# Attention in two halves: full groups for batch 0, groups of 256 queries for batch 1, on one core

## The reference, cut to what matters

```python
# x: 2 x 1024 x 512, eight heads of eight dimensions
qk = (x @ Wqk.T + bqk)             # split into q and k per head
v  = (x @ Wv.T + bv)
scores = q k^T                     # per head, 1024 x 1024
attn = softmax(scores) / 8
x = layernorm(x + (attn v) @ Wo.T + bo)
# feed-forward, int4 weights with a scale for each group of 128 inputs
h = silu(x @ Wg.T) * (x @ Wu.T)    # 512 -> 1792
x = layernorm(x + h @ Wd.T)        # 1792 -> 512
```

## Time and profile before

| | |
|---|---|
| median of 3 runs | 521.45 us (521.42 to 521.49) |
| the profiled execution | 521.81 us, its span 519.7 us |
| granted clock of TensorE, mean | 0.998 |
| PE busy | 501.1 us (96%), 2976 matmuls |
| DVE busy | 413.0 us (79%) |
| ACT busy | 405.5 us (78%) |
| POOL busy | 255.7 us (49%) |

### The profile page before, as it was taken

One profiled execution on the slowest core, in us unless ns is written; L12 is line 12 of the kernel. 1 busy time (PEld: TensorE's weight loads), 2 busy tenths in 40 slices (PEclk: granted clock), 3 DMA queues, 4 the chain that ended last, 5 costly groups with the idle time before them and its releaser, 6 DMA issues.

```text
span 519.7 us, 8086 instructions
## 1 busy us (share of the span) xinstructions
PE 501.1 (96%) x2976; PEld 193.2 (37%) x2976; DVE 413.0 (79%) x705; ACT 405.5 (78%) x558; POOL 255.7 (49%) x295
## 2 busy tenths in 40 slices
PE   8899999999999999999999999999999999999994
PEld 3222222323222322234444444444444444444441
DVE  3699999989999997368878778778668666788677
ACT  1522888998899989877888888888888888888880
POOL 9100091823100715073464676664997962648741
PEclk9999999999999999999999999999999999999999
DMA  6410018576530005700031121140020020000022
GB/s 192 136 68 5 21 35 211 182 144 125 91 59 1 3 5 103 276 7 1 1 59 24 20 43 21 20 62 1 1 81 1 0 83 0 3 0 1 0 81 81
DMA packets 30151, 29.20 MB, mean 56 GB/s; under 512 B 19489, under 2 KB 21921, under 8 KB 29857
## 3 DMA queue, kind: packets, MB, share of 16 engines
q1 hardware_dynamic: 26688, 22.67, 15.7%
q0 software_dynamic: 3424, 6.03, 6.3%
HBM read 24.37 MB, written 4.23 MB: 55 GB/s over the span
## 4 chain that ended last, share of the span: by engine, by line
PE 79%; DVE 7%; POOL 5%; ACT 5%; issue 2%; DMA 1%; SPq 0%; DVEq 0%; POOLq 0%; ACTq 0%
PE ps L1123 16%; PE ps L1135 16%; PE ps L1157 16%; PE ps L1068 9%; PE ps L1039 6%; PE ps L963 6%; DVE mxh L1249 4%; ACT pbuf L760 3%; PE ps L892 3%; POOL x L617 2%; PE ps L1051 1%; PE ps L902 1%; PE ps L1016 1%; POOL stack L663 1%; DMA arena<-xT 1%
## 5 line engine op out<-in xcount | busy, mean ns | idle before, releaser
L1249 DVE TENSOR_REDUCE mxh<-ps 128x1 f32<-128x512 f32 x256 | 157.0, 680 | 6.5 <-PE ps L963 5.3
L760 ACT ACTIVATE pbuf<-ps,gamma 128x1024 f32<-128x1024 f32 x128 | 140.5, 1114 | 16.2 <-PE ps L1039 11.2
L841 ACT ACTIVATE ps<-ps,ratio 128x512 f32<-128x512 f32 x168 | 106.5, 659 | 40.4 <-PE ps L1123 37.3
L1157 PE MATMUL ps<-wd,stack 128*128 128x512 f16 x440 | 129.7, 379 | 0.7 <-POOL stack L663 0.6
L1123 PE MATMUL ps<-arena,wg 128*128 128x512 f16 x448 | 115.5, 379 | 0.1
L1135 PE MATMUL ps<-arena,wu 128*128 128x512 f16 x448 | 115.3, 379 | 0.1
L1423 DVE TENSOR_TENSOR ps<-ps,stack 128x512 f32<-128x512 f32 x128 | 87.8, 695 | 33.4 <-PE ps L1157 31.7
L847 ACT ACTIVATE ps<-ps,ratio 128x512 f32<-128x512 f32 x156 | 98.9, 659 | 6.6 <-PE ps L1135 2.3
L661 POOL CAST stack<-pbuf 128x512 f16<-128x512 f32 x55 | 33.5, 609 | 76.5 <-DVE pbuf L1398 76.5
L1423 DVE TENSOR_TENSOR ps<-ps,pbuf 128x512 f32<-128x512 f32 x76 | 52.6, 695 | 23.2 <-PE ps L1157 22.5
L1068 PE MATMUL ps<-pbuf,arena 128*32 128x256 f32 x832 | 66.5, 391 | 1.7 <-ACT avt L767 1.7
(11 more groups left out here) (120 smaller groups left out, 387.4 us busy)
## 6 DMA issues: line engine op xcount, KB each, us to landing
arena<-xT SPq DMA_DIRECT2D x16, 256.0 KB, 5.8
x<-x SPq DMA_DIRECT2D x2, 2048.0 KB, 10.0
out<-x SPq DMA_DIRECT2D x3, 1024.0 KB, 4.2
stack<-down_ratios SPq DMA_DIRECT2D x1, 2048.0 KB, 9.6
wg<-gq POOLq DMA_DIRECT2D x4, 448.0 KB, 7.3
wu<-uq POOLq DMA_DIRECT2D x4, 448.0 KB, 7.4
wd<-dq POOLq DMA_DIRECT2D x2, 896.0 KB, 10.3
pbuf<-down_ratios SPq DMA_DIRECT2D x1, 1536.0 KB, 6.2
```

Of the source, the lines that this page charges most:

```text
L760: nc.scalar.activation(pbuf[:, pi % 4, :].rearrange("p (a n) -> p a n", a=2), ps[:, at:at + 2, :], ACT.Exp, scale=gamma[:, n // (ALL // B) ...
L841: nc.scalar.activation(gbank[t % 2], gbank[t % 2], ACT.Copy, scale=gr[:, t % G, c:c + 1])\
L1157: mm = nc.tensor.matmul(bank[k], mparts[:, a, t % NM, k * P:(k + 1) * P], wd[:, i, :], start=(i == 0 and a == 0), stop=(a == 1), skip_grou ...
L1249: nc.vector.tensor_reduce(mxh[:, f % 2, qh, half:half + 1], ring_bank("first", n), AX.X, ALU.max)\
```

## The change

Batch 0's blocks keep groups of 512 queries with eight steps. The blocks of batch 1 are cut into groups of 256 queries with four steps, each of two key blocks, so there are 12 groups, and four more turns M and copies by `av_out`. `avt` is still transposed once for 512 queries (TURNS = 8), at steps 9, 17, 25, 34, 42, 50 and 58. From step 24 the first pass issues 3.5 units a step, one unit instead of two in the second pair of even steps; it ends with step 56, and `DRAIN` is 57. Narrow scores are four matmuls of 256 columns for two of 512. `av_whole` is replaced by two halves. The maxima of a group move in four DMAs instead of two, each with fewer rows. avT of the seventh turn is no longer aside but in the shared banks.

The guards and products of the scales go to GpSimd, the reciprocals stay on VectorE at steps 48 and 52. Block 0's statistics are taken in steps 38, 43, 46 and 51, its aggregation in step 52. The second bias is added in four operations, the down weights are loaded in two groups' places, and the residual products stand in periods 26, 27, 33 to 35 and 40 to 44.

```diff
-FG = HG * BT * 2
-FIRST = NB * NG * FG
+WIDE = [(u, g, 0, BT) for u in range(NB // 2) for g in range(NG)]
+NARROW = [(u, g, q, BT // 2) for u in range(NB // 2, NB) for g in range(NG) for q in (0, BT // 2)]
+GROUPS = WIDE + NARROW
+NF = len(GROUPS)
+TURNS = NB * NG
+UNIT0 = [sum(2 * HG * group[3] for group in GROUPS[:f]) for f in range(NF + 1)]
+STEP0 = [sum(2 * group[3] for group in GROUPS[:f]) for f in range(NF + 1)]
+FG = UNIT0[1]
+FIRST = UNIT0[NF]
 AHEAD = FG + 14
+SLOWER = STEP0[3]
...
+        def issued_before(n, pair):
+            return min(AHEAD + 4 * n + 2 * pair - max(0, n - SLOWER + 1) // 2, FIRST)
+
         def firsts_at(n, pair):
-            m = AHEAD + 4 * n + 2 * pair
-            return range(m, min(m + 2, FIRST))
+            return range(issued_before(n, pair), issued_before(n + pair, 1 - pair))
...
-            f, r = divmod(n + 3, KT)
-            if r == 0 and f < NB * NG:
-                return [("M", f, 0)]
-            f, r = divmod(n - 9, KT)
-            if r == 0 and 0 <= f < LASTF:
-                return [("avT", f, 0)]
+            if n + 3 in STEP0[1:NF]:
+                return [("M", STEP0.index(n + 3), 0)]
+            if n in AVT_AT:
+                return [("avT", AVT_AT.index(n), 0)]
...
-        DRAIN = ALL - 11
-        ASIDE = {DRAIN: ("attT", 1, 0), DRAIN + 1: ("wo", 1, 0), DRAIN + 3: ("wo", 1, 1), DRAIN + 4: ("avT", LASTF, 0),
-                 DRAIN + 6: ("attT", 2, 0), DRAIN + 7: ("wo", 2, 0), DRAIN + 9: ("wo", 2, 1)}
+        STATS0_AT = (38, 43, 46, 51)
+        AVT_AT = (9, 17, 25, 34, 42, 50, 58)
+        DRAIN = ALL - 7
+        ASIDE = {DRAIN: ("attT", 1, 0), DRAIN + 1: ("wo", 1, 0), DRAIN + 2: ("wo", 1, 1), DRAIN + 3: ("attT", 2, 0),
+                 DRAIN + 4: ("wo", 2, 0), DRAIN + 5: ("wo", 2, 1)}
...
-        RESIDUAL_AT = 28
+        RESIDUAL_AT = (26, 27, 33, 34, 35, 40, 41, 42, 43, 44)
...
-                for jj in range(2):
-                    r = ROWS * jj + MROW
-                    sp.dma_start(qs[b][r:r + 3, k, 2 * g:2 * g + 2, :],
-                                 mrows[6 * BT * jj:6 * BT * (jj + 1), f % 2, :]).then_inc(s_mld[g], 16)
+                for c in range(HG):
+                    r, t = ROWS * (c // 2) + MROW, 2 * g + c % 2
+                    sp.dma_start(qs[b][r:r + 3, k, t, q * P:(q + count) * P],
+                                 mrows[3 * count * c:3 * count * (c + 1), f % 2, :]).then_inc(s_mld[f % 4], 16)
...
-            for f in range(2, NB * NG):
+            for f in range(2, NF):
                 split_max(f)
                 if f == 2:
-                    add_bias(0)
-                if f in (2, 3, 4):
-                    load_weights(f)
-                if f == 6:
-                    add_bias(1)
+                    add_bias(0, N // P)
                 if f == 3:
                     for t in range(BT):
                         add_attention(0, t)
+                if f == 4:
+                    guard_scales()
+                if 5 <= f < 9:
+                    add_bias(N // P + 2 * (f - 5), 2)
+                if f in (2, 3, 4, 5):
+                    load_weights(f)
+                if f == 8:
+                    guard_down_scales()
+                if f == 9:
+                    scale_ratios()
+                if f == 10:
+                    down_ratios()
...
-                for j in range(2):
-                    rows, t = slice(ROWS * j, ROWS * (j + 1)), 2 * g + pair
-                    mm = nc.tensor.matmul(bank[at + j], ks[b][rows, t, kt * P:(kt + 1) * P],
-                                          qs[b][rows, k, t, :], start=True, stop=True)
+                for i in range(BT // count):
+                    kt = BT // count * (n - STEP0[f]) + i
+                    for j in range(2):
+                        rows, t = slice(ROWS * j, ROWS * (j + 1)), 2 * g + pair
+                        mm = nc.tensor.matmul(bank[at + j][:, i * own:(i + 1) * own], ks[b][rows, t, kt * P:(kt + 1) * P],
+                                              qs[b][rows, k, t, q * P:(q + count) * P], start=True, stop=True)
...
-                av_whole(n - 1)
-            av_whole(ALL - 1)
+                for half in range(2):
+                    av(n - 1, half)
+            for half in range(2):
+                av(ALL - 1, half)
...
+                if n in STATS0_AT:
+                    attention_stats(0, STATS0_AT.index(n))
+                if n == 48:
+                    invert_scales()
+                if n == 52:
+                    invert_down_scales()
+                    mean_variance(0)
             att_out(1)
-            down_ratios()
+            apply(0, range(2))
+            normalise(TURNS - 2)
             for t in range(2):
                 add_output(1, t)
-            apply(0)
-            scale_ratios()
+            apply(0, range(2, BT))
             for t in range(2, BT):
                 add_output(1, t)
-            normalise(LASTF)
             att_out(2)
```

More of the change, by code:

```diff
@@ L317, in wait_aside_read @@
         def wait_aside_read(engine, use):
[L319 to L322, removed]
+            engine.wait_ge(s_aside, copy_count[use])
         def wait_attT(engine, u):
@@ L439, in max_rows @@
             def max_rows(f):
-                u, g = divmod(f, NG)
+                u, g, q, count = GROUPS[f]
                 if f:
@@ L557, in split_max @@
             def split_max(f):
[L559 to L561 removed]
+                n = HG * GROUPS[f][3]
+                part = [mp[:, f % 2, 0:3 * n].rearrange("p (c i q) -> p i c q", c=HG, i=3)[:, i, :, :] for i in range(3)]
+                top = mx[:, f % 2, 0:n].rearrange("p (c q) -> p c q", c=HG)
+                rest = mres[:, 0:n].rearrange("p (c q) -> p c q", c=HG)
                 pool.wait_ge(s_mxc, f + 1)
@@ L591, in load_weights @@
                         pool.dma_start(wu[:, c, :], uq[c]).then_inc(s_gu, 16)
[L592 to L595, removed]
+                if f > 3:
+                    own = slice((f - 4) * G // 2, (f - 3) * G // 2)
+                    pool.dma_start(wd[:, own, :], dq[own].rearrange("g p n -> p g n")).then_inc(s_dq, 16)
             split_max(0)
@@ new lines, in guard_scales, with guard_down_scales, scale_ratios @@
+            def guard_scales():
+                pool.wait_ge(s_sc, 32)
+                guard(scales[:], small[:], s_raw)
+            def guard_down_scales():
+                pool.wait_ge(s_ds, 32)
+                guard(both, tiny, s_draw)
+            def scale_ratios():
+                pool.wait_ge(s_inv, 1)
+                own, after, to = [tile[:].rearrange("p (a n) -> p a n", n=C) for tile in (scales, small, ratio)]
+                nc.gpsimd.tensor_tensor(to[:, :, 0:C - 1], own[:, :, 0:C - 1], after[:, :, 1:C], ALU.mult)\
+                  .then_inc(s_ratio, 1)
@@ L1063, in av @@
                     pe.wait_ge(s_vc, 2 * B)
-                if kt == 0 and n:
-                    pe.wait_ge(s_ave, n // KT)
-                lo, hi = half * TB // 2, (half + 1) * TB // 2
+                if step == 0 and n:
+                    pe.wait_ge(s_ave, f)
+                lo, width = half * TB // 2, TB // 2
+                if count == BT:
+                    kt, to = step, lo
+                    first = step == 0 and half == 0
+                else:
+                    kt, to = 2 * step + half, q * P
+                    first = kt == 0
                 for j in range(HG):
-                    mm = nc.tensor.matmul(bank[AVB][j * VC:(j + 1) * VC, lo:hi], vst[b][:, kt, g * HG + j, :],
-                                          pbuf[:, (2 * n + j // 2) % 4, (j % 2) * TB + lo:(j % 2) * TB + hi],
-                                          start=(kt == 0 and half == 0), stop=(kt == KT - 1), skip_group_check=True)
+                    at = (j % 2) * TB + lo
+                    mm = nc.tensor.matmul(bank[AVB][j * VC:(j + 1) * VC, to:to + width], vst[u * TB // N][:, kt, g * HG + j, :],
+                                          pbuf[:, (2 * n + j // 2) % 4, at:at + width],
+                                          start=first, stop=(kt == KT - 1), skip_group_check=True)
                 mm.then_inc(s_av, 1)
@@ L1356, in _ @@
                     row_maxima(1, 0)
-            for n in range(ALL):
+            for n in range(DRAIN):
                 if n == 1:
```

164 lines of the change are left out of this document (77 added, 87 removed).

## The result

The changed kernel takes **524.05 us** (median of 4 runs, 523.89 to 524.22), the kernel before 521.43 us beside it (521.18 to 521.49). The ratio is 1.0051, 95% interval 1.0034 to 1.0069: slower by half a per cent, where 523.8 us was forecast. The profiled execution took 523.89 us with a span of 522.1, against 521.81 and 519.7 before.

A forecast was written before the change was run, and what follows sets the result against it. VectorE was taken to bound steps 24 to 56, with TensorE's sequence right behind. Steps 24 to 56 +0.1, drain +2.8, feed-forward -0.6 sum to +2.3 us on 521.45: 523.8 us, range 519.6 to 527.0.

The forecast's parts named there:

- The floor, 81.3 us: Steps 24 to 56: TensorE's own sequence, 66 pairs at 1.11 us plus turns M, avT and group copies, sums to 81.3 us.
- The three unknown costs, 2.1 us: Steps 24 to 56: costs the earlier trace doesn't show, (a) 0.5, (b) 1.2 and (c) 0.4 us on top of the floor.
- (a): Batch 1's scores as four matmuls of 256 columns, 50 pairs: 0.01 us a pair, 0.5 us, at most 3.5.
- (c): SyncE issues four maxima DMAs for two: groups without avT wait 0.1 us for them, 0.4 us in all.
- (b): Three-bank first-pass ring: VectorE's statistics or reciprocals between reductions hold TensorE, 0 to 3 us, taken as 1.2.
- The drain: Steps 57 to the last A (attention-times-V): all six asides now lie there, 18.7 us against 15.91, +2.8, bounds +0.9 to +3.5.
- Feed-forward part: Behind the attention loop: moved residual products remove TensorE's only wait on GpSimd there, -0.6 us.
- The floor is all there is: Rival, whole kernel: costs (a) to (c) are nothing and the drain is bare work, -1.7 us, 519.8 us; chance 0.22.
- Gain and drain cancel: Rival: half of (a) to (c) and a drain of +1.9 without the wait, +0.3 us, 521.7 us; chance 0.20.
- The maxima land late: Rival, attention loop: the fourth DMA lands 0.6 us later, eight narrow groups wait, +4.8 us, 528.6 us; chance 0.10.
- VectorE stays the bound: Rival, steps 24 to 56: VectorE needs 83 us instead of 76, giving 523 us; no separate chance.
- The rule about the shared port: VectorE's combine blocked by GpSimd's SBUF work: eight groups at 0.9 us, 7 us more; no chance of its own.

The follow-up runs named there:

- a_light: Changed kernel with first-pass reductions from unit 142 on over 256 of 512 keys: 521.80 us, ratio 1.0006 to the kernel before.
- b_light: Kernel before with first-pass reductions from unit 142 on over 256 of 512 keys: 517.58 us, ratio 0.9923.
- b_scores4: Kernel before with only batch 1's scores as four matmuls of 256 columns in place of two of 512: 521.86 us, ratio 1.0006.
- b_dma4: Kernel before with only a group's maxima moved by four DMAs in place of two: 521.32 us, ratio 0.9993.
- a_order: Changed kernel with VectorE adding block 1's first two outputs ahead of normalise of the seventh turn: 523.46 us, ratio 1.0032 to the kernel before.
- b_resid: Kernel before with only the residual products moved to periods 26, 27, 33 to 35 and 40 to 44: 520.70 us, ratio 0.9981.
- a_resid28: Changed kernel with the residual products back in periods 28 to 37: 525.58 us, ratio 1.0076 to the kernel before.
- a_rate4: Changed kernel with the first pass at four units a step throughout, ending with step 52: 530.26 us, ratio 1.0173 to the kernel before.
- a_rate4_deep: As a_rate4, with four buffers in place of two for the combined maxima and their parts: 530.18 us, ratio 1.0164 to the kernel before.
- a_rate4_bias: As a_rate4, with add_bias's four quarters moved from behind groups 5 to 8 to behind groups 7 to 10: 526.33 us, ratio 1.0085 to the kernel before.

## Why the prediction was right, point by point

**VectorE stops being the bound** (right). 77.71 us busy of 83.81, forecast 76, at most 80. The reductions of steps 24 to 56 were 71.87 us in 116, not 68.4 in 114: one that stands alone counts 0.68 and only the following ones of a run 0.60, and at a pace of 1.11 more stand alone.

**The floor, 81.3 us** (right). a_light shows 81.54. M at 0.49 over, the full copies at 0.53 to 0.54 for 0.44, the narrow copies at 0.32 for 0.23, avT at 0.58 to 0.59 are in the trace as priced or within 0.1. Only five of the six narrow copies fall into this stretch; the sixth delays step 57. The 2.0 us by which this floor lies under 83.28 were never the gain of the change over its own floor before: that was 79.40, by b_light.

**The three unknown costs, 2.1 us** (their sum right, the split wrong, which is luck). They are 83.81 - 81.54 = 2.3 us. (a) 0.5 for narrow scores: b_scores4 shows no more than its interval allows, -0.0004 to +0.0015 of the time, and 0.06 us in its stretch. (c) 0.4 for maxima that land late: one wait of 0.4 us where the weight load's own queue takes as long, and b_dma4 costs nothing. The prediction set beside (c) a fixed cost of about 2.0 us from the Trainium skill, DMA: Bandwidth & Descriptors, section Anatomy of one DMA. That section describes DMAs that GpSimd issues. These are issued by SyncE, and no run here turns on the 0.2 us between 2.0 and the 2.22 of the trace. (b) 1.2 for VectorE's inserts: the places beside them hold 1.4, of which some 0.3 may be the reductions' own (twice 0.14), so this term was sized about right. The step that failed is one that the sum put at nothing: VectorE's reductions alone, 0.9 us, since the prediction compared 114 x 0.60 with the whole stretch and not the three two-unit pairs in a row with the ring. Inserts beside a turn or copy cost nothing that is seen: the reciprocal of 0.84 us at 178.62 lies there, and the pairs around it are those of a_light.

**Steps 24 to 56**: +0.1 forecast, +0.53 measured, 0.2 by the floor and 0.2 by these costs (by b_light and a_light, -1.6 from VectorE and +2.1 from the rest).

**The drain**: +2.8 forecast, +3.40 measured. By steps, forecast and measured: 57 2.88, 3.09; 58 3.3, 3.19; 59 3.05, 3.31; 60 2.05, 2.02; 61 and 62 4.80, 5.09; 63 2.60, 2.61. The wait of wo for add_output was 0.64 us for 0.65, by the chain foreseen (avT, normalise, two added outputs), and a_order took it away. Steps 57, 59 and 62 are 0.2 to 0.3 us longer than priced, the others within 0.1; these 0.76 us make the whole miss of 0.6. Step 59's 0.26 belongs to the wait, for in a_order the step takes 2.40, the price of a step with wo. Step 62 has the second wait that the prediction only named as a bound: wo (2, 1) starts 0.15 us behind the added outputs of wo (2, 0), in the changed kernel and, with the same 2.69 us for the step, in a_order. In step 57 ScalarE copies a narrow group (0.38 us, at 199.34) ahead of the exponential that M waits for, which step 53 of the kernel before, the source of the price of 2.88, hadn't. These two are read from the trace and weren't tried.

**Feed-forward part**: -0.6 forecast, -1.0 measured. The mechanism is shown by b_resid (-1.0) and a_resid28 (+1.3 to 1.5 when undone). The size was off because I counted only what the waits name; the stretch from the first to the last down matmul fell by 0.98 us, of which the wait is 0.6. What the other 0.4 is stays open.

**The rivals.** *The floor is all there is*: fell, VectorE costs 2.3 us over the floor. *Gain and drain cancel*: fell, mostly for the drain, 19.31 where it needed 17.8; even without the wait, in a_order, it is 18.40, so the lower bound of 16.8 was 1.6 too low. *The maxima land late*: fell, by b_dma4 and by the single wait. *VectorE stays the bound*: fell.

**The rule about the shared port**, which I gave no chance of its own, was the nearest miss. In the changed kernel no combine met add_bias, 0.166 to 0.176 us each; at 4 units a step, where the combines come earlier against GpSimd's queue, two of twelve did and cost 3.9 us. I had ruled it out because combine runs before GpSimd has anything to do for its own group. That reason was wrong: GpSimd has the quarters of the bias queued behind its wait for landed rows, and they start whenever that wait ends. The changed kernel escapes by timing, not by design.

**Luck.** 524.05 lies 0.25 us from the forecast of 523.8, closer than its parts: the drain was 0.6 too low, steps 24 to 56 0.4 too low, the feed-forward part 0.4 too high, and the profiled execution began 0.53 us earlier.

## What to carry to other kernels

Smaller tiles that relieve one engine bring a fixed number of turns and copies per tile to all of them: price the two as separate sums, since here VectorE's cost fell by 1.6 us and the rest grew by 2.1, and neither is seen in the total. An engine with 6 us to spare in 84 can still cost 2.3: 1.4 where extra work comes in lumps longer than the buffer ahead of it covers, 0.9 where its main work is spread unevenly, so compare it with the pace over as few pairs as the buffer holds, and not over the stretch; a trial with its main work halved shows this where the busy shares don't. When a small operation shows ten times its length, look at what the neighbour engine ran until the moment it ended.

## What was not expected of the hardware

An operation of VectorE on 8 columns with two SBUF inputs took 2.00 and 1.82 us in place of 0.17, to the end of a GpSimd operation of 2.35 us with two SBUF inputs. Behind the second of these stalls the granted clock of TensorE fell as well: in a_rate4 it was 0.87 in the 3.5 us of the stall and 0.63, so in part at the lower level of 1.2 GHz, in the 3.4 us behind it, in which TensorE worked without a break (windows with the columns of the earlier trace rows):

```profile
151.70:155.20 3.50, 1.94 (x20) 0.51 (x18) 3.50 (x5) 1.64 (x3) 3.19 (x6) 0.87 1.18 186
155.20:158.60 3.40, 3.40 (x33) 1.01 (x33) 2.23 (x4) 2.02 (x3) 1.39 (x1) 0.63 0.40 67
158.60:162.00 3.40, 3.10 (x34) 1.14 (x34) 3.40 (x7) 3.25 (x4) 0.00 (x0) 1.00 0.11 19
```

TensorE was busy 1.94 of the 3.50 us of the stall. In a_rate4_deep the matching stretches (150.30 to 153.80, and from there to 157.20) have 0.97 and 0.53. Behind the first stall of each, where TensorE was busy 1.66 and 1.64 of 3.40 us, the clock stayed at 1.00, so such a stall alone doesn't bring the fall; what tells the two apart stays open. The two pairs behind this stall took 2.03 and 1.34 us, where a_rate4_bias has 1.61 and 1.11 at the same turn. With the stalled pairs themselves (3.24 for 1.55, 3.45 for 1.40) that makes 1.69 + 2.05 + 0.65 = 4.39 us, which is the difference of the two stretches, 90.49 - 86.07 = 4.42: the stall and the clock behind it are all of it. (The profiled execution of a_rate4, 532.16 us, is the longest of its four; by the medians the difference is 3.9.)
